# Expert products of a mixture-of-experts layer: another order of the same matmuls over the PSUM banks

## The reference, cut to what matters

```python
xn = layernorm(x)                                    # (8, 1024, 256)
affinity = softmax(xn @ gate_w)                      # 8 experts
gating, index = top_k(affinity_T, K=256)             # 256 rows per batch and expert
x_sel = xn[b, index]
g = einsum('bekd,edi->beki', x_sel, Wg)              # d = 256, i = 512
u = einsum('bekd,edi->beki', x_sel, Wu)
h = silu(g) * u
out = einsum('beki,eid->bekd', h, Wd)
x_out = zeros.at[b, index].add(out * gating)
result = x + attention(xn) + x_out
```

## Time and profile before

| | |
|---|---|
| median of 3 runs | 1675.8 us (1673.33 to 1677.91) |
| profiled execution | 1677.62 us, its span in the trace 1675.8 us |
| TensorE busy, of the span | 97% |
| VectorE, ScalarE, GpSimd busy | 72%, 74%, 30% |
| expert stage | from 1114 us to the end, about 562 us |

### The profile page before, as it was taken

How to read it: one execution, slowest core, us unless ns; L and a number is a source line. 1 busy time by engine, 2 the same in 40 slices (tenths; PEclk the granted TensorE clock), 3 DMA queues, 4 the chain that set the end, 5 groups by cost and what they waited for, 6 DMA issues and landing times.

```text
span 1675.8 us, 28807 instructions
## 1 busy us (share of the span) xinstructions
PE 1620.3 (97%) x10880; PEld 926.5 (55%) x10880; DVE 1204.2 (72%) x2463; ACT 1237.2 (74%) x1513; POOL 502.2 (30%) x480
## 2 busy tenths in 40 slices
PE   6799999999999999999999999988999999999997
PEld 5234344444434434434434443347888888888886
DVE  9775566576576567657656658869888888888883
ACT  5698998998898899899898899963444444444443
POOL 3121121111111112112112100034566656565653
PEclk9799999999999999999999999999999999999998
DMA  5645653684584486366376366344444435444433
GB/s 184 167 100 118 146 134 82 177 146 109 124 183 128 109 168 155 93 154 163 95 146 150 76 159 147 67 140 87 109 95 72 98 67 100 102 64 101 67 62 37
DMA packets 113987, 196.06 MB, mean 117 GB/s; under 512 B 20896, under 2 KB 59680, under 8 KB 113696
## 3 DMA queue, kind: packets, MB, share of 16 engines
q1 hardware_dynamic: 83696, 143.01, 36.6%
q0 software_dynamic: 29040, 49.83, 15.4%
q10 hardware_dynamic: 1088, 1.05, 0.2%
HBM read 117.27 MB, written 76.55 MB: 116 GB/s over the span
## 4 chain that ended last, share of the span: by engine, by line
PE 81%; DVE 5%; ACT 5%; DMA 4%; issue 2%; SPq 1%; POOL 1%; POOLq 0%; DVEq 0%; ACTq 0%
PE o_ps L1101 23%; PE score L1180 20%; PE score L1087 16%; PE side L971 5%; PE score L1192 5%; ACT probs L869 5%; PE o_ps L1192 3%; PE side L1192 2%; PE side L1012 2%; PE side L981 2%; DMA o_sums<-o_sb 1%; DMA k_parts<-parts 1%; DMA base<-in_x 1%; PE side L951 1%; DVE cos_sb L1528 1%
## 5 line engine op out<-in xcount | busy, mean ns | idle before, releaser
L869 ACT ACTIVATE probs<-score 128x1024 f32<-128x1024 f32 x1024 | 964.2, 1052 | 95.9 <-PE score L1087 89.8
L1101 PE MATMUL o_ps<-probs,v_ones 128*32 128x512 f32 x4096 | 513.9, 602 | 1.7 <-DVE o_sb L1593 1.1
L1087 PE MATMUL score<-q_stack,k_stack 50*128 50x512 f32 x2048 | 376.7, 449 | 9.7 <-issue 4.4
L1087 PEld LDWEIGHTS score<-q_stack,k_stack 50*128 50x128 f32 x2048 | 166.4, 185 | 336.9 <-ACT probs L869 300.6
L762 POOL DMA_INDIRECT out<-probs,rot x128 | 201.0, 1571 | 195.0 <-ACT probs L859 166.1
L1528 DVE STREAM_TRANSPOSE cos_sb<-qk 32x256 f32<-32x256 f32 x496 | 216.2, 436 | 9.1 <-DMA qk<-xn_rows,rot 1.0
L848 ACT ACTIVATE probs<-score 128x512 f32<-128x512 f32 x128 | 76.5, 598 | 193.7 <-PE score L1180 192.4
L1101 PEld LDWEIGHTS o_ps<-probs,v_ones 128*32 128x32 f32 x4096 | 97.1, 108 | 211.5 <-issue 147.2
L737 POOL TENSOR_TENSOR square<-qk 128x512 bf16<-128x512 f32 x56 | 71.0, 1298 | 341.5 <-DVE qk L1379 341.5
L1180 PE MATMUL score<-k_stack,zn_hi 128*128 128x512 f32 x512 | 142.3, 394 | 9.0 <-DVE probs L1542 9.0
L751 POOL DMA_INDIRECT qk<-xn_rows,rot x128 | 128.3, 1003 | 38.3 <-issue 29.5
(11 more groups left out here) (271 smaller groups left out, 2372.2 us busy)
## 6 DMA issues: line engine op xcount, KB each, us to landing
q_parts<-parts SPq DMA_DIRECT2D x16, 1024.0 KB, 5.1
k_parts<-parts SPq DMA_DIRECT2D x16, 1024.0 KB, 8.5
q_stack<-q_parts SPq DMA_DIRECT2D x62, 256.0 KB, 6.2
k_stack<-k_parts SPq DMA_DIRECT2D x62, 256.0 KB, 8.3
q_stack<-q_parts SPq DMA_DIRECT2D x66, 128.0 KB, 6.1
k_stack<-k_parts SPq DMA_DIRECT2D x66, 128.0 KB, 7.3
o_sums<-o_sb SPq DMA_DIRECT2D x256, 32.0 KB
num<-o_sums SPq DMA_DIRECT2D x32, 256.0 KB
```

Source lines behind the costliest of these rows:

```text
L869: act.activation(probs[probs_of(b, s)][:, 2 * i:2 * i + 2, :], score[ring_of(b, p)][:, :, :], ACT.Exp, scale=SCALE).then_inc(exp_done, 1)
L1087: last = pe.matmul(score[ring_of(b, p)][:, w, :], k_stack[par][rows, i, kt * P:(kt + 1) * P], q_stack[par][rows, i, qh * HALF:(qh + 1) * H ...
L1101: last = pe.matmul(o_ps[j * KEYS_W:(j + 1) * KEYS_W, :], v_ones[par][:, kt, j, :], probs[probs_of(b, s)][:, j, :], start=kt == 0, stop=kt ...
```

## The change

The same matmuls are issued with the same operands; their number does not change. In `gate_up` the loop over gate and up is now the innermost: each gate matmul is followed by the up matmul with the same part and chunk of x. In `down` the loop over the four row tiles is innermost: for each chunk f and kind of part the four tiles follow one another. All four tiles' banks must be free before the first matmul of `down`: it waits for `y_scaled` of the whole unit before, and in units 1 and 2 for both jobs' `side_free`. Only in the last unit is the last chunk done tile by tile.

```diff
--- before.py
+++ after.py
@@ -1174,39 +1174,37 @@
             pe.wait_ge(x_split, splits_of(unit))
             for f in range(FC):
                 need(pe, h_done, FC * unit + f - 1)
-                for w, bank, full in ((GATE, g_ps, gate_full), (UP, u_ps, up_full)):
-                    for i, (wt, xt) in enumerate(((we_hi, x_hi), (we_lo, x_hi), (we_hi, x_lo))):
-                        for c in range(DC):
+                for i, (wt, xt) in enumerate(((we_hi, x_hi), (we_lo, x_hi), (we_hi, x_lo))):
+                    for c in range(DC):
+                        for w, bank, full in ((GATE, g_ps, gate_full), (UP, u_ps, up_full)):
                             last = pe.matmul(bank[f % 2], wt[k][w][:, c, f * P:(f + 1) * P], xt[:, c, :],
                                              start=i == 0 and c == 0, stop=i == 2 and c == DC - 1)
-                    last.then_inc(full, 1)
+                            if i == 2 and c == DC - 1:
+                                last.then_inc(full, 1)
 
         def down(unit):
             k = unit // UNITS % 2
 
-            def part(t, fs):
-                at = slice(t * P, (t + 1) * P)
-                for f in fs:
-                    pe.wait_ge(h_split, FC * unit + f + 1)
-                    for i, (ht, wt) in enumerate(((h_hi[:, f, at], we_hi), (h_lo[f][:, at], we_hi), (h_hi[:, f, at], we_lo))):
-                        last = pe.matmul(rows_ps(t)[:, 0:D], ht, wt[k][DOWN][:, f, :],
+            def part(f, tiles):
+                pe.wait_ge(h_split, FC * unit + f + 1)
+                for i, (ht, wt) in enumerate(((h_hi[:, f, :], we_hi), (h_lo[f], we_hi), (h_hi[:, f, :], we_lo))):
+                    for t in tiles:
+                        last = pe.matmul(rows_ps(t)[:, 0:D], ht[:, t * P:(t + 1) * P], wt[k][DOWN][:, f, :],
                                          start=i == 0 and f == 0, stop=i == 2 and f == FC - 1)
-                return last
-
-            for t in range(ST):
-                need(pe, y_scaled, ST * (unit - 1) + t + 1)
-                for job in END_JOBS:
-                    if END_BANKS[job] == (unit, t):
-                        pe.wait_ge(side_free, end_jobs.done(job))
-                part(t, range(FC - 2))
+                        if i == 2 and f == FC - 1:
+                            last.then_inc(down_full, 1)
+
+            need(pe, y_scaled, ST * unit)
+            for job in END_JOBS:
+                if END_BANKS[job][0] == unit:
+                    pe.wait_ge(side_free, end_jobs.done(job))
+            for f in range(FC - 1):
+                part(f, range(ST))
             if unit + 1 < E * UNITS:
+                part(FC - 1, range(ST))
+            else:
                 for t in range(ST):
-                    part(t, (FC - 2,))
-                for t in range(ST):
-                    part(t, (FC - 1,)).then_inc(down_full, 1)
-            else:
-                for t in range(ST):
-                    part(t, (FC - 2, FC - 1)).then_inc(down_full, 1)
+                    part(FC - 1, (t,))
 
         pe.wait_ge(exp_done, NB * PAIRS - NPAIR)
         turn_first()
```

## The result

The changed kernel takes 1681.1 us (median of 12 runs, 1679.55 to 1683.12). The kernel before takes 1677.2 us in the same session (12 runs, 1673.33 to 1679.32). The ratio is 1.0026 [1.0017, 1.0035]: slower by 4.4 us by the ratio, 3.9 by the medians. That is more than the noise and still within 0.3%. The profiled execution took 1682.46 us with a span of 1680.6, and before its span was 1675.8: +4.8 us. The forecast had +2.2.

What follows compares the result with a forecast made beforehand. TensorE was taken as the bound, its matmul count times their pace. Terms of 0 pace, 0 hand-over, +1.06 tail and +1.12 unit 2 wait gave +2.2 us on the 1675.8 median: 1678.0 us, range 1673.5 to 1683.5.

Steps and rivals of the forecast that it cites:

- Bank changes, 0 ns each: In gate, up and down, changing banks at nearly every matmul was taken to cost nothing, within about 3 ns per change.
- Pace term: Time per TensorE matmul in gate, up and down: taken as unchanged, 0 us, bounded at 7 us either way.
- The rival by which alternate banks shorten the gap: Matmuls of all units would speed up to bare columns, saving 38 us, to about 1640 us; chance 7%.
- the Trainium skill's figure: Isolated warm matmul gap, N / 2.4 + 2.5 ns; if repeated bank use caused the excess, 31 us saved, 1647 us.
- Hand-over: Later gate results delay silu by 1.14 us and VectorE's product by 0.38, hidden behind TensorE's work: 0 us, 0.9 cover.
- The rival that it becomes the bound: Late silu would make chunk 2's low part miss its down matmul in 29 units: 29 us, 1707 us; chance 8%.
- Tail: Last unit's tile 0 is complete 9 down matmuls later, so the first scatter and the end move by +1.06 us.
- Unit 2's wait: Down's first matmul in unit 2 now waits for VectorE's adds: +1.12 us, with no later idle time to return it.
- The rival by which the waits don't add: Waits in units 1 and 2 would add nothing because VectorE's adds end earlier than thought: 1676.9 us; chance 5%.
- Unit 1's: Down's start in unit 1 waits 1.13 us for VectorE's adds, swallowed by a later 2.23 us wait: 0 us.
- Clock: Half-clock spell after unit 1's long wait could shift by 1.7 us either way; taken as 0; rival 1676.3 or 1679.7, 12%.
- The waits of unit 0: The 0.74 us wait in unit 0 goes, but the following 3.50 us wait grows to about 4.2: 0 us gained.

Runs made afterwards that it cites:

- Gate and up alone: Kernel before with only gate and up interleaved as in the changed kernel, down as before: 1675.97 us against 1675.66, ratio 1.0006.
- mixed order: Changed kernel, but in down the kind of part also changes at every matmul, banks still changing each time: 1677.84 us against 1675.66, ratio 1.0010.
- ends left as they were: Changed kernel with units 1, 2 and the last keeping the earlier order of down: 1680.45 us, ratio 1.0026; in another session 1680.13 us, ratio 1.0018.

## Why the prediction was right in its direction and short by half

- **Bank changes, 0 ns each.** Right. Gate and up alone and the mixed order change banks as often as the changed kernel does, and have the pace of before.
- **Pace term, 0 with a bound of 7 us.** Mis-sized: it was +1.5 us. I asked of the order only what it does to the banks. It also puts matmuls side by side whose weights lie in one tile, eight times where there were at most two, and inside such a run a step is 120 ns instead of 117.8. That costs 0.05 us a unit. The test I made, 24 matmuls against 24 in the earlier trace rows, compared two stretches with the same sequence of operands, so it could not have shown it. The rival by which alternate banks shorten the gap, and with it the reading of the Trainium skill's figure that I priced at 31 us, fell: no step of the steady units became shorter. (The figure is in TensorE: Matmul & The Clock Gate, section Back-to-back issue gap.)
- **Hand-over, 0.** Right, with its sizes: silu 1.13 us later (1.14 forecast), product 0.36 (0.38), 0.9 us of cover left. The rival that it becomes the bound fell with that.
- **Tail, +1.06.** Right: 1.07.
- **Unit 2's wait, +1.12.** The wait came in its size, 1.17 us (1.33 by starts), in all five executions with the new order. Its net cost was overrated: I took the 2.23 us wait at chunk 2 only as idle time that swallows unit 1's, and not as one that can have a spell at half clock behind it. With the spells counted, unit 2 costs 0.35 us more on the mean, 15.49 for 15.15. The one trace that I had of before had no spell there, so it couldn't show this. The rival by which the waits don't add fell in its reason, for the adds end no earlier; in its effect it was near. **Unit 1's** wait was swallowed, as forecast (23.39 us for 23.55 in the mixed order).
- **Clock, 0 within 1.7.** The mechanism stood there, the size was wrong: +0.96 between the two profiled executions, 0.9 to 1.4 between the means of the 14. I took the middle of a range where a longer wait could cut both ways. The runs lean one way: in unit 1, 4.5 us of waiting cost more than 3.5, and about 2 cost nothing.
- **The waits of unit 0.** 0.74 us was not the third largest wait of the stage, as the prediction has it: the trace of before has waits of 2.19, 1.13 and 1.42 us in unit 0 too. No term of the sum rests on it.

With the terms as the runs show them on the mean the sum is 1.5 (pace) + 0.9 to 1.4 (clock in unit 1) + 1.07 (tail) + 0.35 (unit 2) = 3.8 to 4.3 us, against 3.9 to 4.4 measured. The mixed order removes only the first of them, which leaves 2.3 to 2.8; 1.7 to 2.2 was measured, with a bound of 3.0. With the ends left as they were it is 2.4 to 2.9, and 3.0 to 4.6 was measured. That the forecast fell short by half and not by more owes something to luck: it had unit 2 too high by 0.8 and the pace and the clock too low by 2.4 to 2.9.

Settled: that the operands' order and place cause the slower steps, not the banks; and in the traces the tail. Not settled: what the waits of units 1 and 2 cost net of the clock, which rests on how 14 executions fall; and why the kernel with its ends left as they were isn't faster than the changed one. Open: what in the addresses decides the pace. A shift of 4096 bytes changes nothing, one of 1664 or 128 changes the single steps, and the one rule that I could state fell.

## What to carry to other kernels

When an order of matmuls changes, write down for each neighbouring pair what changes: the bank, but also where the weights and where the moving rows come from; two stretches of the old trace test a cost only if they differ in it. A loop order that makes all destinations needed at once moves every wait for them to the front, and completes them all at the end: price both at the first and last unit, where nothing covers them. A wait of TensorE that seems free, since another is taken away ahead of it, can still be paid for in the clock behind it, and a new wait can be paid back when it shortens a later one with such a spell. One trace of before shows one outcome of the clock: look at several executions before you price a difference of 1 or 2 us by it.

## What the runs showed of the hardware

- With a weight load for every matmul, the pace at the full clock was 226.7 ns for 512 columns, behind the first five steps of a unit, and 117.5 to 118.3 for 256, behind the first three, as long as in `down` no more than two matmuls running took their weights from `parts`. It was so whatever the order of banks: one bank 3 or 6 times running, or another each time (before, gate only, mixed kinds).
- Where the tiles lie in SBUF to one another changes the pace of single matmuls of 256 columns between 113 and 123 ns. With `parts` and the tiles behind it shifted by 1664 bytes, 48 matmuls of 512 columns took 11.10 us in place of 10.91 with even experts, in one and the same program otherwise.
- In unit 1 no spell at half clock followed a TensorE wait of about 2 us (three executions); after 3.5 us one followed in three of four, and after 4.5 us the time to the next restart was 1.2 to 2.8 us longer than without one in all seven. In unit 2 a spell of 1.6 us followed a wait of 2.23 us in six executions of nine, the two of one program differing, and none followed 0.6 us in five. So the length of the wait alone did not decide.
- One program, measured in two sessions on two chips, was 3.0 and 4.3 us over before by ratio, with five rounds each. A claim on less than that 1.3 us needs the trace.
